# Splitting attention weights in place, three mean passes in the head, and ScalarE as a second reader of the mask words

## The chip, the cores and the metric

The kernel runs on 1 core of one Trainium2 chip. The metric is the device time of one execution in microseconds; the times are given as the median of several executions, and one more execution was taken with the hardware profiler. TensorE is called PE, VectorE DVE, ScalarE ACT, GpSimd POOL and SyncE SP, as in the profile.

## The reference

Two graph attention layers over N = 4096 nodes with F = 64 features and one dense 4096 x 4096 integer adjacency matrix, nearly empty (the diagonal and about one entry in a thousand):

```python
def layer(h, a, slope):                   # layer 2 first does h = h @ W
    e = (h @ a[:64])[:, None] + (h @ a[64:])[None, :]
    e = leaky_relu(e, slope)              # 0.01 in layer 1, 0.2 in layer 2
    p = softmax(where(adj > 0, e, -9e15), axis=1)
    return p @ h                          # layer 2 adds elu() on this
x = layernorm(x + layer1(x)); out = layernorm(x + layer2(x))
```

## The kernel before

The exponential of a leaky sum is a product of a factor of the row and a factor of the column, one pair of factors for positive sums and one for negative ones. So each layer is a product of a 0/1 matrix (mask and sign) with weighted feature rows, done once for each sign and combined per row. The matrix is made from signs: ACT writes sign(s_i + d_j) as one byte, DVE masks it with an AND (`negative`, L831) and an XOR (`positive`, L842).

**Tiling.** A supertile `q` is 512 rows (4 tiles `t` of 128), and there are `NQ` = 8 of them in each layer. A step `k` (8 in each supertile) takes 4 chunks `b` of 128 columns. In a step, ACT makes four rows of signs (`compare`, L670), DVE does `negative` and `positive`, and PE does 32 matmuls (`products`, L1223): 4 tiles by 4 chunks by 2 signs, each with a 128x128 fp8 stationary block and a moving block of 195 bf16 columns. PE accumulates a whole supertile in four PSUM banks `acc`.

Layers and supertiles are counted from 1 in the text and steps, groups and tiles from 0; the code counts all from 0, so its `weigh(1, 0)` is group 0 of layer 2.

**Words.** In layer 1 the adjacency has to be turned first. POOL issues its loads (L490) into `enc`, PE turns one step's four blocks into the PSUM tile `tb` (`turn_masks`, L1147), two steps ahead and in the middle of `products`, and DVE copies them to `mask_t` (`extract`, L757), one step ahead. Layer 2 finds all words in `mask_t`. `look` (L742) checks the words for values that are not 0 or 1.

**Weights.** Chunk values `val` (64 features and a one) are multiplied by the column's two factors to 520 f32 products for each group of four chunks, by POOL (`multiply`, L328), for group 7 of layer 2 by DVE. Each product is kept as three bf16 parts. The f32 word's upper half is the first part; DVE subtracts it (`weigh`, L814), the rest's upper half is the second part, and DVE subtracts that and writes the third part (L820). ACT copies the first two (`keep_parts`, L626, one copy of 1040 bf16; POOL's L554 for the last group). All three land side by side in `wmov`, in the order sign, part, column; this is what the matmuls read. The products lie in scratch (`split` and borrowed places) that two groups share in turn, so `multiply` waits for DVE and ACT two groups back. Group g of layer 2 may be written to `wmov` only when the last supertile of layer 1 has done step g (`mm_done`). Two groups are made earlier, staged in the unused end of `mask_t` and moved by two DMAs of SP (`move_weights`, L456); `extract` in the last supertile waits for these before it writes over the end.

**Queues.** Every engine runs a list written out by hand. In supertile 1 of layer 1, DVE's step k is: `negative(k)`, `positive(k)`, `extract(k+1)`, the two halves of `weigh(k+1)`, then small work: `sum_s` at k = 1, `set_scur` at k = 2, `clip_s` at k = 4. POOL's `multiply(g)` there waits for `positive(g-2)`, counted by `poss`. PE's mean of x (`mean_pass`, L1262) is one matmul of 512 f32 columns in the middle of steps 1, 2, 4 and 5 each; DVE reduces the result (`take_mean`, L908) in step 0 of supertile 2. A supertile's sums are read from PSUM by DVE (`sum_parts`, L857) in step 0 of the next one; the epilogue after them is POOL's, and DVE's at the change of layers. `positive(k)` waits until step k-2 is done on PE (two buffers), `compare(k)` for k-4 (four buffers).

Of the kernel before, what the change touches and what calls it, by code (L numbers as in the profile page):

```python
# [5 lines left out]
P = 128  # L6
N = 4096
F = 64
NQ = 8
TI = 4  # L10
KB = 8
NB = 4
ROWS = TI * P
KP = 2
# [3 lines left out]
FD = F + 1  # L18
# [13 lines left out]
STAGED = 2  # L32
# [3 lines left out]
WEIGH = 2  # L36
XP = 4
MEAN_STEPS = (1, 2, 4, 5)
# [14 lines left out]
def fast_attention(nc, x, adj, a0, w1, a1, x1_dram, out, flag, stored):  # L53
# [7 lines left out]
    with ExitStack() as ctx:  # L61
# [12 lines left out]
        enc = sb("enc", [P, NU, TI, UW], F32)  # L74
# [3 lines left out]
        wmov = sb("wmov", [P, KB * NB, 2 * WC], BF16)  # L78
        vsum = sb("vsum", [P, 2, F], F32)
        val = sb("val", [P, KB * NB, FD], F32)  # L80
        split = sb("split", [P, NB, 2, 2, FD], F32)
# [5 lines left out]
        ones = sb("ones", [P, 1], F32)  # L87
        share = sb("share", [P, 1], F32)
# [12 lines left out]
        strange = sb("strange", [P, 1], F32)  # L101
# [9 lines left out]
        def spare(q, half):  # L111
# [8 lines left out]
        s_prod, d_prod, x_chunks = spare(NQ - 1, 1), spare(NQ - 2, 0), spare(NQ - 2, 1)  # L120
# [28 lines left out]
        moved = [sem(f"moved{i}") for i in range(STAGED)]  # L149
        looked = sem("looked")  # L150
        turned = sem("turned")
        masked = sem("masked")
        rows_turned = sem("rows_turned")
# [14 lines left out]
        w_prod = [sem(f"w_prod{i}") for i in range(2)]  # L168
        w_vec = sem("w_vec")
        w_act = sem("w_act")  # L170
        w_pool = sem("w_pool")
# [35 lines left out]
        lots = NB * 2 * 2 * FD  # L207
        other_split = [flat[:, 0:lots].rearrange("p (b s r c) -> p b s r c", b=NB, s=2, r=2) for flat in (
            mask_t[:, NQ - 3].rearrange("p k t i -> p (k t i)").bitcast(F32),
            enc[:, 1:3].rearrange("p u t j -> p (u t j)"))]  # L210

        last_words = mask_t[:, NQ - 1].rearrange("p k t i -> p (k t i)").bitcast(F32)
        staged_split = last_words[:, 0:lots].rearrange("p (b s r c) -> p b s r c", b=NB, s=2, r=2)
        staged_words = last_words.bitcast(BF16)
        first_staged = 2 * KB * TI * P - STAGED * NB * 2 * WC

        def staged(g):

            c0 = first_staged + g * NB * 2 * WC
            return staged_words[:, c0:c0 + NB * 2 * WC]  # L220

        def steps_of(g):

            c0 = first_staged + g * NB * 2 * WC
            return range(c0 // (2 * TI * P), (c0 + NB * 2 * WC - 1) // (2 * TI * P) + 1)

        def is_staged(layer, g):
            return layer == 1 and g < STAGED

        def parts_of(layer, g):  # L230

            if g % 2 == 0:
                return split[:, :, :, :, :]
            return staged_split if is_staged(layer, g) else other_split[layer]

        def weights_of(layer, g):

            if is_staged(layer, g):
                return staged(g).rearrange("p (b c) -> p b c", b=NB)
            return wmov[:, NB * g:NB * g + NB]  # L240

        def top_of(layer, g):

            return parts_of(layer, g).rearrange("p b s r c -> p (b s r c)").bitcast(BF16)\
                .rearrange("p (b s r c h) -> p b s r c h", b=NB, s=2, r=2, h=2)[:, :, :, :, :, 1]

        lone_mean = enc[:, 0, 0, :].rearrange("p (t d) -> p t d", d=F)
        enc8 = enc[:, :, :, :].bitcast(FP8)
# [61 lines left out]

        def multiply(eng, ops, layer, g):

            n = NQ * layer + g
            cs = slice(NB * g, NB * g + NB)
            if layer == 1:

                eng.wait_ge(grp_set, 3 * (g + 1))
                eng.wait_ge(b_set, 4 if g < EARLY else 2 * (g - EARLY) + 6)
                if g % 2 and not is_staged(1, g):
                    eng.wait_ge(turned, KB * (NQ - 1) + 6)  # L320
            elif g:

                eng.wait_ge(poss, max(g - 1, 1))

            if n > 1:
# [1339 lines left out]
```

## Time and profile before

| | |
|---|---|
| median of 3 executions | 437.58 us (437.0 to 438.23) |
| the profiled execution's own time | 437.87 us |
| its span from first to last instruction | 436.0 us |
| busy in the span: PE / DVE / ACT / POOL | 406.4 / 380.3 / 382.9 / 252.2 us |
| granted TensorE clock, mean | 0.992 |

The span is the part that the profile shows; 1.87 us of the execution lie around it. A busy share alone does not say what bounds a stage, because the stages differ: the head and the change of layers have work that the steady supertiles don't have.

### The profile page before, as it was taken

To read this page: it belongs to the slowest core of one execution; us is meant where nothing else is said; L and a number is where in the kernel's file an instruction comes from. 1 tells how busy PE (TensorE), PEld (TensorE's weight loads), DVE (VectorE), ACT (ScalarE), POOL (GpSimd) and SP (SyncE) were. 2 spreads that over 40 slices of the span, in tenths; PEclk is the share of its full clock that TensorE was granted. 3 is DMA by queue.
4 is the path that set the end of the run, shared out by engine and by line. 5 is a ranking of instruction groups with operands and counts; after the bars stand their busy time and mean duration, and the time that the engine had idled before them with its cause. 6 is when DMAs were issued, how large, how long until landed. Compare 5 with 4: busy or idle time off the path is not lost.

```text
span 436.0 us, 11844 instructions
## 1 busy us (share of the span) xinstructions
PE 406.4 (93%) x4484; PEld 397.8 (91%) x4484; DVE 380.3 (87%) x683; ACT 382.9 (88%) x590; POOL 252.2 (58%) x292
## 2 busy tenths in 40 slices
PE   1599999999999999999999999999999999999980
PEld 1388999999999999999998998999999999999980
DVE  4799998899898989999889997689999999999963
ACT  3899986979979799779998989999999999999930
POOL 5533353753738547296493135568696969695931
PEclk9999999999999999999999999999999999999996
DMA  5999989799897998988610000000000000000000
GB/s 118 99 107 108 90 75 98 68 101 80 78 102 66 95 85 73 90 73 88 83 52 1 2 26 2 2 26 2 27 2 26 0 24 1 24 2 26 2 26 17
DMA packets 22766, 22.48 MB, mean 52 GB/s; under 512 B 1344, under 2 KB 22464, under 8 KB 22720
## 3 DMA queue, kind: packets, MB, share of 16 engines
q0 software_dynamic: 17424, 16.78, 44.4%
q1 hardware_dynamic: 4208, 4.05, 2.9%
q10 hardware_dynamic: 1088, 1.05, 0.7%
q8 instruction: 28, 0.46, 0.4%
q14 instruction: 18, 0.15, 0.1%
HBM read 69.30 MB, written 2.10 MB: 164 GB/s over the span
## 4 chain that ended last, share of the span: by engine, by line
PE 75%; DVE 15%; issue 6%; POOL 1%; DMA 1%; ACT 0%; DVEq 0%; POOLq 0%
PE acc L1223 67%; PE tb L1147 5%; DVE neg L831 3%; DVE pos L842 3%; DVE mask_t L757 2%; PE srcb L1157 1%; DMA mask_t<-in_x 1%; DVE split L814 1%; DVE mask_t L814 1%; PE pg L1191 1%; DVE scr L857 1%; DVE wmov L820 1%; DVE mask_t L913 1%; DVE dcol L921 1%; DVE enc L814 1%
## 5 line engine op out<-in xcount | busy, mean ns | idle before, releaser
L670 ACT ACTIVATE neg<-srcb,dcol 128x512 int8<-128x512 f32 x512 | 358.2, 973 | 4.4 <-PE acc L1223 4.0
L1223 PE MATMUL acc<-wmov,pos 128*128 128x195 bf16 x2016 | 357.1, 248 | 3.6 <-DVE pos L842 2.6
L1223 PE MATMUL acc<-wmov,neg 128*128 128x195 bf16 x2016 | 357.3, 249 | 0.0
L1223 PEld LDWEIGHTS acc<-wmov,pos 128*128 128x128 fp8e4 x2016 | 198.5, 98 | 7.6 <-DVE pos L842 5.6
L1223 PEld LDWEIGHTS acc<-wmov,neg 128*128 128x128 fp8e4 x2016 | 197.5, 98 | 2.3 <-issue 1.3
L842 DVE TENSOR_TENSOR pos<-neg,mask_t 128x1024 uint16<-128x1024 uint16 x128 | 104.8, 819 | 15.3 <-DVE neg L831 1.6
L831 DVE TENSOR_TENSOR neg<-neg,mask_t 128x1024 uint16<-128x1024 uint16 x128 | 102.9, 804 | 10.8 <-ACT neg L670 8.0
L490 POOL DMA_DIRECT2D enc<-in_adj x31 | 24.7, 798 | 63.5 <-DVE scr L857 31.1
L757 DVE TENSOR_SCALAR mask_t<-tb 128x512 uint32<-128x512 uint32 (+1 forms) x64 | 43.9, 686 | 6.7 <-PE tb L1147 6.0
L1147 PE MATMUL tb<-ident,enc 128*128 128x128 f32 x256 | 39.5, 278 | 2.7 <-DMA enc<-in_adj 2.7
L742 DVE SCALAR_TENSOR_TENSOR odd<-mask_t,odd 128x1024 uint32<-128x1024 uint32 x32 | 38.8, 1213 | 0.0
L857 DVE TENSOR_REDUCE scr<-acc 128x130 f32<-128x390 f32 x60 | 31.7, 557 | 1.4 <-PE acc L1223 0.2
L1147 PEld LDWEIGHTS tb<-ident,enc 128*128 128x128 f32 x256 | 29.1, 143 | 3.5 <-DMA enc<-in_adj 3.3
L345 POOL TENSOR_TENSOR scr<-scr,acol 128x260 f32<-128x260 f32 x14 | 13.0, 926 | 30.0 <-issue 23.3
L404 POOL TENSOR_SCALAR small<-mv 128x4 f32<-128x4 f32 x14 | 9.1, 652 | 19.2 <-DVE mv L875 19.0
L407 POOL TENSOR_TENSOR small<-small 128x4 f32<-128x4 f32 x14 | 19.3, 1382 | 1.2
L328 POOL TENSOR_TENSOR split<-val,bcol 128x520 f32<-128x520 f32 x8 | 9.0, 1125 | 14.5 <-DVE scr L392 12.3
L347 POOL TENSOR_TENSOR scr<-scr,acol 128x260 f32<-128x260 f32 x14 | 14.9, 1065 | 0.0
L366 POOL TENSOR_TENSOR scr<-scr 128x256 f32<-128x256 f32 x14 | 13.5, 963 | 1.1
L421 POOL TENSOR_TENSOR xout<-scr,small 128x256 f32<-128x256 f32 x14 | 13.1, 937 | 1.1
L350 POOL TENSOR_TENSOR scr<-scr 128x260 f32<-128x260 f32 x14 | 13.0, 930 | 1.1
L635 ACT COPY xt<-pg 128x256 f32<-128x256 f32 x8 | 3.4, 421 | 11.0 <-PE pg L1183 11.0
(139 smaller groups left out, 301.7 us busy)
## 6 DMA issues: line engine op xcount, KB each, us to landing
enc<-in_adj POOLq DMA_DIRECT2D x31, 512.0 KB, 8.2
mask_t<-in_x ACTq DMA_DIRECT2D x4, 256.0 KB, 5.7
x_rows<-xout SPq DMA_DIRECT2D x8, 128.0 KB, 3.1
resid<-x_rows SPq DMA_DIRECT2D x8, 128.0 KB, 2.1
out<-xout SPq DMA_DIRECT2D x8, 128.0 KB, 1.7
wmov<-mask_t SPq DMA_DIRECT2D x2, 390.0 KB, 3.4
enc<-in_adj POOLq DMA_DIRECT2D x2, 256.0 KB, 8.3
resid<-in_a SPq DMA_DIRECT2D x1, 64.0 KB, 4.6
```

The lines of the kernel that those rows point to most:

```text
L347: ops.tensor_tensor(tmp, part[:, :, 1, :], wide(acol[:, layer, 1, q, :], FD), ALU.mult)\
L366: ops.tensor_tensor(numf, numf, tmpf, ALU.add).then_inc(done, 1)
L407: ops.tensor_tensor(rstd, var, mhalf, ALU.pow).then_inc(done, 1)
L490: nc.gpsimd.dma_start(enc8[:, u, :, :], adj_v[q, u]).then_inc(adj_landed[u], 16)
L670: ins = nc.scalar.activation(neg[:, k % SR, :, b], srcb[:, q % 2, :], ACT.Sign, bias=dcol[:, layer, c:c + 1])
L742: nc.vector.scalar_tensor_tensor(odd[:, :], mask_pairs[:, n, :], NOT_BINARY, odd[:, :], ALU.bitwise_and, ALU.bitwise_or).then_inc(looked, 1)
L757: nc.vector.tensor_scalar(mask_t[:, q, k, :, :], tb[:, :, :].bitcast(U32), WORD, None, ALU.bitwise_and).then_inc(masked, 1)
L831: nc.vector.tensor_tensor(neg16[:, k % SR, :], neg16[:, k % SR, :], bits, ALU.bitwise_and)\
L842: nc.vector.tensor_tensor(pos16[:, k % MR, :], neg16[:, k % SR, :], bits, ALU.bitwise_xor)\
L857: nc.vector.tensor_reduce(part[:, t, :, :], acc[t][:, 0:2 * WC].rearrange("p (s r c) -> p s c r", s=2, r=SPLIT), AX.X, ALU.add).then_inc(a ...
L1147: ins = nc.tensor.transpose(tb[:, t, :], enc[:, k // KP, t, k % KP * P:(k % KP + 1) * P], ident[:, :])
L1223: ins = nc.tensor.matmul(acc[t][:, side * WC:(side + 1) * WC], m[:, t * P:(t + 1) * P, b], wmov[:, c, side * WC:(side + 1) * WC], start=fi ...
```

## The change

- **In place.** The products of a group get an eight-byte slot each: the f32 product and, beside it, the f32 rest. The slot's four bf16 halves are then: waste, first part, third part, second part. `weigh` writes the third part into the lower half of the rest, and the matmuls read halves 1 to 3 of each slot in place: a moving operand of 65 runs of three bf16 with a step of eight bytes, instead of 195 side by side. In PSUM the order becomes sign, column, part, still without gaps, and `sum_parts` reads three neighbours. `wmov`, `split`, `keep_parts` (ACT, 15 copies), POOL's copy and the two DMAs of SP are gone, and the waits with them. Each group has a home of its own: `wts`, `apart_wts`, the end of `mask_t`, or a slot of `enc_lots` (`wait_for_home` says when a home is free). `weigh(1, 0)` moves from step 4 to step 5 of supertile 7, `weigh(1, 1)` from step 6 of supertile 7 to step 2 of supertile 8, and POOL's `multiply(1, 1)` from step 5 to step 7 of supertile 7.
- **Mean.** The four passes go to bank 1 of `srcb`: one at PE's very start, one before `turn_stat`, one between the first two `turn_masks`, and one in step 1. `take_mean` goes to step 2 of supertile 1; `spread_rows` of supertile 2 waits for it.
- **Words by ACT.** In supertile 1 the words of steps 3, 5 and 7 are copied by ACT right after the signs of the same step, as 1024 uint16 each (before, all were DVE's). Those who wait for words there count two semaphores.

```diff
-                        else:
-                            keep_parts(0, k - 1)
+                        if k in BY_ACT:
+                            extract(k)
...
+            def extract(k):
+
+                act.wait_ge(turned, k + 1)
+                nc.scalar.copy(mask_t[:, 0, k, :, :].rearrange("p t i -> p (t i)").bitcast(U16),
+                               tb[:, :, :].rearrange("p t i -> p (t i)").bitcast(U16)).then_inc(masked_act, 1)
...
-                dve.wait_ge(w_prod[g % 2], n // 2 + 1)
-                nc.vector.tensor_tensor(rest, both[:, :, :, 0, :], top[:, :, :, 0, :], ALU.subtract)\
-                    .then_inc(w_vec, 1)
-                if layer == 1 and not is_staged(1, g):
-
-                    dve.wait_ge(mm_done, KB * (NQ - 1) + g + 1)
+                both, halves = parts_of(layer, g), halves_of(layer, g)
+                product, rest = both[:, :, :, :, 0], both[:, :, :, :, 1]
+
+                dve.wait_ge(w_prod, n + 1)
+                nc.vector.tensor_tensor(rest, product, halves[:, :, :, :, 1], ALU.subtract).then_inc(w_vec, 1)
+
                 dve.wait_ge(w_vec, WEIGH * n + 1)
-                nc.vector.tensor_tensor(w[:, :, :, 2, :], rest, top[:, :, :, 1, :], ALU.subtract)\
+                nc.vector.tensor_tensor(halves[:, :, :, :, 2], rest, halves[:, :, :, :, 3], ALU.subtract)\
...
-                acc[t][:, side * WC:(side + 1) * WC], m[:, t * P:(t + 1) * P, b],
-                                wmov[:, c, side * WC:(side + 1) * WC], start=first, stop=last, skip_group_check=True)
+                acc[t][:, side * WC:(side + 1) * WC].rearrange("p (c r) -> p c r", r=SPLIT),
+                            m[:, t * P:(t + 1) * P, b],
+                                moving(layer, k, b, side), start=first, stop=last, skip_group_check=True)
...
+            def halves_of(layer, g):
+
+                return home(layer, g).bitcast(BF16).rearrange("p (b s c h) -> p b s c h", b=NB, s=2, h=4)
+
+            def moving(layer, g, b, side):
+
+                return halves_of(layer, g)[:, b, side, :, 1:4]
...
+            def mean_pass(h):
+
+                pe.wait_ge(x_landed[h], 16)
+                ins = nc.tensor.matmul(srcb[:, 1, :], share[:, :].broadcast_to([P, P]),
+                                       x_chunks[:, h * piece:(h + 1) * piece], start=h == 0, stop=h == XP - 1)
```

## Rows read from the trace of the kernel before

**Rows 1.** The page's costliest groups: busy, mean ns, idle before and its releaser.

```profile
L1223 PE MATMUL acc<-wmov,pos 128*128 128x195 bf16 x2016 | 357.1, 248 | 3.6 <-DVE pos L842 2.6
L857 DVE TENSOR_REDUCE scr<-acc 128x130 f32<-128x390 f32 x60 | 31.7, 557 | 1.4 <-PE acc L1223 0.2
```

**Rows 2.** Busy time of the engines by stretch (length, then PE, PEld, DVE, ACT, POOL).

```profile
24.00:54.00 30.00, 29.87 (x305) 27.28 (x302) 28.81 (x46) 28.84 (x42) 10.33 (x12) 1.00 1.08 101
224.00:263.00 39.00, 36.44 (x401) 34.62 (x399) 35.96 (x69) 36.36 (x62) 13.07 (x15) 1.00 0.04 12
266.00:415.00 149.00, 148.96 (x1716) 148.55 (x1715) 134.59 (x223) 148.29 (x222) 112.13 (x115) 1.00 0.04 12
```

**Rows 3.** The chain that ended last: start, us, what.

```profile
56.48 1.05 DVE pos L842
...
274.62 22.14 PE acc L1223 x256
```

**Rows 4.** Timeline of DVE, supertile 1 and the start of supertile 2.

```profile
27.28 0.69 DVE L842 TENSOR_TENSOR pos<-neg,mask_t 128x1024 uint16<-128x1024 uint16 x1
27.89 0.68 DVE L757 TENSOR_SCALAR mask_t<-tb 128x512 uint32<-128x512 uint32 x1
28.49 1.20 DVE L814 TENSOR_TENSOR mask_t<-mask_t 128x520 f32<-128x520 f32 x1
29.72 0.70 DVE L820 TENSOR_TENSOR wmov<-mask_t 128x520 bf16<-128x520 f32 x1
...
51.69 0.68 DVE L908 TENSOR_REDUCE meanv<-pg 128x64 f32<-128x512 f32 x1
...
55.29 1.09 DVE L831 TENSOR_TENSOR neg<-neg,mask_t 128x1024 uint16<-128x1024 uint16 x1
56.48 1.03 DVE L842 TENSOR_TENSOR pos<-neg,mask_t 128x1024 uint16<-128x1024 uint16 x1
```

**Rows 5.** Timeline of POOL in the same stretch.

```profile
28.07 1.06 POOL L328 TENSOR_TENSOR split<-val,bcol 128x520 f32<-128x520 f32 x1 [0.79 <-DVE pos L842]
...
55.22 0.61 POOL L363 TENSOR_TENSOR scr<-small,meanv 128x256 f32<-128x256 f32 x1
55.91 1.06 POOL L366 TENSOR_TENSOR scr<-scr 128x256 f32<-128x256 f32 x1
```

**Rows 6.** Timeline of PE in the head.

```profile
12.57 0.37 PE L1163 MATMUL pg<-ident,stat 128*1 128x128 f32 x1 [1.61 <-DVE stat L765]
...
22.16 0.80 PE L1147 MATMUL tb<-ident,enc 128*128 128x128 f32 x4 [0.53 <-DMA enc<-in_adj]
...
26.01 1.02 PE L1262 MATMUL pg<-mask_t,share 128*128 128x512 f32 x2
26.87 0.25 PE L1223 MATMUL acc<-wmov,pos 128*128 128x195 bf16 x1
...
54.12 0.26 PE L1223 MATMUL acc<-wmov,pos 128*128 128x195 bf16 x1 [0.25 <-DVE pos L842]
```

**Rows 7.** Timeline of ACT in the head.

```profile
33.63 1.07 ACT L626 COPY wmov<-split 128x1040 bf16<-128x1040 bf16 x1
```

**Rows 8.** Timeline of DVE at the change of layers.

```profile
220.53 0.69 DVE L757 TENSOR_SCALAR mask_t<-tb 128x512 uint32<-128x512 uint32 x1 [0.53 <-PE tb L1147]
224.16 0.69 DVE L757 TENSOR_SCALAR mask_t<-tb 128x512 uint32<-128x512 uint32 x1 [0.38 <-PE tb L1147]
233.26 1.23 DVE L814 TENSOR_TENSOR split<-split 128x520 f32<-128x520 f32 x1
259.10 1.57 DVE L820 TENSOR_TENSOR wmov<-enc 128x520 bf16<-128x520 f32 x1
```

**Rows 9.** Timeline of POOL and PE at the change of layers.

```profile
232.87 1.07 POOL L328 TENSOR_TENSOR enc<-val,bcol 128x520 f32<-128x520 f32 x1 [2.88 <-ACT wmov L626]
259.06 1.06 POOL L554 COPY wmov<-enc 128x1040 bf16<-128x1040 bf16 x1 [7.22 <-DVE enc L814]
262.41 0.26 PE L1223 MATMUL acc<-wmov,pos 128*128 128x195 bf16 x1 [0.54 <-DVE pos L842]
```

More of the change, by code:

```diff
@@ L86, in fast_attention @@
         ident = sb("ident", [P, P], F32)
-        ones = sb("ones", [P, 1], F32)
-        share = sb("share", [P, 1], F32)
+        single = sb("single", [P, 3], F32)
+        ones, share, strange = (single[:, i:i + 1] for i in range(3))
         att1 = sb("att1", [F, 2], F32)
@@ L167, in fast_attention @@
         a_set = sem("a_set")
-        w_prod = [sem(f"w_prod{i}") for i in range(2)]
+        w_prod = sem("w_prod")
         w_vec = sem("w_vec")
-        w_act = sem("w_act")
-        w_pool = sem("w_pool")
         limits = sem("limits")
@@ L236, in weights_of @@
[L236 to L248, printed above, removed]
+        first_tail = KB * TI * P - TAIL * LOT
@@ new lines, in home, with wait_for_home @@
+        def home(layer, g):
+            if layer == 0 and g < TAIL:
+                flat = last_words[:, first_tail + g * LOT:first_tail + (g + 1) * LOT]
+            elif layer == 0:
+                flat = wts[:, g - TAIL]
+            else:
+                flat = {0: apart_wts[:, :], 1: enc_lots[:, 0], 2: enc_lots[:, 1], 3: wts[:, 0], 4: wts[:, 1],
+                        5: wts[:, 2], 6: enc_lots[:, 2], 7: enc_lots[:, 3]}[g]
+            return flat
+        def wait_for_home(eng, g):
+            if g in (1, 2, 6, 7):
+                lot = {1: 0, 2: 1, 6: 2, 7: 3}[g]
+                eng.wait_ge(turned, KB * (NQ - 1) + KP * (lot + 1))
+            elif g:
+                eng.wait_ge(mm_done, KB * (NQ - 1) + g)
@@ L309, in before, with wait_for_words @@
             return layer, q - 1, NQ * layer + q - 1
+        def wait_for_words(eng, n):
+            if isinstance(n, int) and n <= KB:
+                by_act = sum(k < n for k in BY_ACT)
+                eng.wait_ge(masked, n - by_act)
+                if by_act:
+                    eng.wait_ge(masked_act, by_act)
+            else:
+                eng.wait_ge(masked, n - len(BY_ACT))
         def multiply(eng, ops, layer, g):
-            n = NQ * layer + g
             cs = slice(NB * g, NB * g + NB)
@@ L906, in take_mean @@
                 dve.wait_ge(mean_ps, layer + 1)
-                shares = pg[:, :] if layer == 0 else pg[:, 0:2 * F]
+                shares = srcb[:, 1, :] if layer == 0 else pg[:, 0:2 * F]
                 nc.vector.tensor_reduce(meanv[:, :], shares.rearrange("p (c f) -> p f c", f=F), AX.X, ALU.add)\
@@ L997, in body @@
                         sum_parts(*done, range(0, TI // 2))
-                    if ahead(layer, q, k, 1):
+                    if ahead(layer, q, k, 1) and not (layer == 0 and is_first(q) and k + 1 in BY_ACT):
                         extract(*ahead(layer, q, k, 1))
@@ L1025, in body @@
                             sum_s(1, 2, 2)
+                        if k == 2:
+                            take_mean(0)
                         if k == 4:
@@ L1200, in products @@
                 apart(pe, q)
[L1201 to L1204 removed]
+                if is_first(q):
                     pe.wait_ge(w_vec, WEIGH * (NQ * layer + k + 1))
[L1207 to L1210 removed]
                 for t in range(TI):
```

149 lines of the change are left out of this document (43 added, 106 removed).

## The prediction, on record before the changed kernel was run

> **What bounds the kernel now.** I read the page's groups first. A matmul of `products` has a mean of 248 ns [rows 1], but matmuls overlap, so their pace is read elsewhere: in the chain 256 of them take 22.14 us [rows 3], which is 86.5 ns each. There are 2 x 8 x 8 x 32 = 4096 of them, 354 us of a span of 436. Busy time by stretch says where PE is not the bound [rows 2]: from 266 to 415 us it idles 0.04 us in 149, but from 224 to 263, the change of layers, 2.56 us in 39. The steady supertiles give nothing unless the matmul itself gets faster or slower.
>
> The head is less plain. From 24 to 54 us PE is busy for 29.87 of 30 us [rows 2], yet the chain runs on DVE up to a `positive` that ends at 57.53 [rows 3] and only then turns to PE. Both hold: PE has four mean passes there, and DVE ends each `positive` only shortly before PE is free. At 54.12 PE is the one that waits, 0.25 us for DVE [rows 6]. So the head has two bounds almost level, and taking work off one gains only what the other allows.
>
> DVE's own step in the head is lengthened by POOL. After `positive(2)` (end 27.97) come `extract` (0.60 from start to start), then L814, which starts at 28.49 and takes 1.20 us, then L820, 0.70 [rows 4]. POOL's `multiply` runs from 28.07 to 29.13 [rows 5]. L814 ends at 29.69, 0.56 after POOL: it was held until POOL was done. Two instructions later in the head show the turn-taking. `negative` at 55.29 ends at 56.38, 0.55 after L363's end; L366, wanted from 55.83, ends 0.59 after `negative`; `positive`, wanted from 56.48, ends 0.54 after L366 [rows 4, 5]. DVE with two inputs in SBUF and POOL alternate, each holding the other off for a whole instruction, even where DVE's next instruction follows within 0.1 us. `extract` reads PSUM and isn't held (0.68 us under a running POOL).
>
> **The change, part by part.** The sum is made against the profiled execution, 437.87 us; the median of the three is 0.29 lower.
>
> *The moving operand.* No row shows one with gaps. From below the cost is nothing; a gain is excluded, since the columns stay 195. From above: the operand now crosses 65 x 8 = 520 bytes instead of 390, so if bytes crossed set the pace, 86.5 becomes 115.3 ns and 4096 matmuls cost 118 us more. The nearest row is TensorE's other read: the stationary block takes one byte of every four, so it crosses 512 bytes in each 86.5 ns, and it keeps up (its column PEld has as many instructions as PE, [rows 2]). I take nothing. The Trainium skill (SBUF — State Buffer, section Door 1: The DMA port swizzle) says that SBUF is read in lines of 16 bytes and that two or more reads in a line keep full rate, so that bf16 may step up to 8 elements for free; here a line gives six of its eight halves. By that rule the term is 0 as well, where the bound by bytes says 118 us; no run here shows it yet.
>
> *DVE's operands* get steps of eight bytes. Nothing in the rows has that form either. L814 now runs 520 elements in about 0.61 us, one element a cycle, and already reads every other half; I take no change. The bound from above is doubling: 0.6 us for each of two halves of 16 groups, of which the groups on the path (8 in the head, 5 at the change) would cost 15 us. `sum_parts` reads neighbours instead of a step of 65; its 557 ns for 390 elements [rows 1] is again about one a cycle, so 0.
>
> *ACT.* Each copy that leaves is 1.07 us [rows 7], 15 in all with eight in the head. What comes is three copies of 1024 elements from PSUM, about 1.1 us each by the same row. ACT gets 8 x 1.07 - 3 x 1.1 = 5.3 us lighter in the head, and none of that is on the path: `negative` isn't waiting for signs there. `extract(3)` on ACT must wait for PE's turn in the middle of step 1 (26.2), ends near 27.3, and its words are wanted by `negative(3)` at 30.4. What is queued behind it on ACT is `compare(4)`, done by 30.2 and wanted at 34.3. Covered; were ACT late, each copy would cost its 1.1.
>
> *DVE in the head.* Three extracts leave: 3 x 0.60 = 1.80 at steps 2, 4 and 6. But at steps 2 and 4 `multiply(4)` and `multiply(6)` are released by the `positive` just before, and the extract was the cover for 0.6 us of it. Without it: L814 from 27.99 to 28.60, POOL's turn to 29.6, L820 to 30.2, where today it ends at 30.34. That is 0.1 instead of 0.6, twice. At step 6 no multiply is left, and the full 0.6 comes. Sum 0.8. Against it: `negative` of steps 3 to 7 waits for a third semaphore. A gap between DVE instructions grows from about 0.02 to 0.08 with a second wait (28.49 + 1.20 to 29.72, against `negative` to `positive`, 56.38 to 56.48, [rows 4]), so 5 x 0.05 = 0.25. `take_mean` costs 0.60 at step 2 and gives back 0.60 in supertile 2 (51.69, [rows 4]), both on DVE's chain. DVE's net at 57.5: 0.8 - 0.25 = 0.55 earlier.
>
> *PE in the head.* A pass is 0.86 us (26.01 to 26.87, [rows 6]). Three leave the stretch: 2.58. The one before `turn_stat` lies in the 1.61 us that PE idled before 12.57 [rows 6]. Even at twice its later length, 1.7 us, it would end 0.1 after that idle; PE's small matmuls there may also run faster for the work before them and give 0.1 back; I take 0. The pass between the first turns is hidden: what is late there is the adjacency's DMA, for which PE waits again at 22.16 [rows 6]. With 2.58 less, PE stands free at each `positive` from step 2 on, and DVE alone decides: head 0.55 to 0.65 faster. I take **0.6**.
>
> *The change of layers.* `weigh(1, 1)` moves into supertile 8 at step 2: 0.62 + 0.62 = 1.24, and 0.4 for one POOL turn (its epilogue runs there). DVE idles 0.53 at 220.53 and 0.38 at 224.16 for PE's turns [rows 8], and without two ACT copies in supertile 7 it starts the supertile some 0.25 earlier. So 1.64 - 1.16 = 0.48 late. `multiply(1, 5)` no longer waits 2.88 us for ACT's copy [rows 9]; it comes right behind `multiply(1, 4)` and holds L820 of group 3 for about 0.87, where today it holds L814 of group 4 for 0.54 (1.23 at 233.26, [rows 8]): 0.33 late. Four L820 lose a second wait, 4 x 0.06 = 0.24 early. At the end POOL's copy goes: it held L820 of group 7 for 0.87 (1.57 at 259.10, [rows 8, 9]), and PE idled 0.54 before 262.41 [rows 9]. The two adds behind it (0.6 each) move up to 256.8 and can hold L328, at most 0.5. So 0.54 back. Sum 0.48 + 0.33 - 0.24 - 0.54 = +0.13, against a bound of -2.56 if all of PE's idling went. SP's two DMAs and the waits for them go too: they landed long before `extract` asked. The new waits of `extract` in supertile 8 (its steps 0 and 1 done) are met by two steps.
>
> Sum: 437.87 - 0.6 + 0.1 = 437.4 for a profiled execution, **437.1** as a median.
>
> **The rivals.** *DVE keeps its turn.* If L820, 0.02 us behind L814, goes ahead of the waiting POOL, steps 2 and 4 save 1.1 each. With step 6 that is 2.8, less 0.6 until the mean is given back; then PE's own work bounds the head, and its 2.58 is the most it can give. About 2.2: 437.87 - 2.2 + 0.1 - 0.29 = 435.5. For it: the gap is smaller than the 0.1 of the pair above. Against it: POOL took its turn in those rows every time. Chance 0.24.
>
> *DVE has no slack in supertile 8.* The 1.16 us of absorption don't come, because POOL's epilogue is late by as much as it is held, and DVE waits for it instead. Then 1.64 + 0.33 - 0.24 - 0.54 = +1.2 there, less 0.6: 438.2. It ends above before as soon as more than 0.6 arrives at PE. For it: PE idles 2.56 us in 224 to 263 because DVE is the chain there. Chance 0.17.
>
> *The gaps in the moving operand cost.* Each ns is 4.1 us; half a ns outweighs all else. The bound is 437.6 + 118 = 555. Chance 0.06.
>
> *Nothing comes.* The head gives nothing because the early waits (mean before `spread_rows`, the words' two counts) take it back: 437.6. Chance 0.08.
>
> **How the numbers follow.** My forecast has 0.45. What a measurement here can tell from no change is 0.3%, 1.3 us. Faster by more: the first rival and a little of the forecast's lower end, 0.28. Slower by more: the operand's 0.06 and the upper half of the second rival, 0.15. Within: 0.57. The range runs from 435.0 (first rival, with a few tenths of the idle at the change) to 438.8 (second rival with a POOL turn more); only the operand's case and the far ends lie outside, under 2 in 10. The forecast's own range is 436.4 to 437.8.
>
> **What would show it.** Matmuls of `products` 86.5 ns apart in the steady supertiles (not so: the third rival). At steps 2 and 4 of supertile 1, L820 about 1.65 us long behind a short L814 (0.7 would be the first rival). One mean pass of 0.86 us in step 1 and none later; PE idling a few tenths before several steps of supertile 1. The first full PE stretch of layer 1 starting at about 57.0 instead of 57.5. In supertile 8, DVE's idling of 0.53 and 0.38 gone, PE's idling at about 229 and 236 grown by tenths, and no idling before step 7 of supertile 9. Wrong would be above all: a turn order between DVE and POOL unlike that of [rows 4, 5], or slower two-input instructions through the eight-byte steps.

## The result and the profile after

The changed kernel takes 535.29 us (median of 4 executions, 534.82 to 536.22), the one before 437.29 beside it: a ratio of 1.223 [1.220, 1.226], slower by 98 us. I had forecast 437.1. The case that came is the third rival, the gaps in the moving operand, which had 0.06. The profiled execution took 536.22 us with a span of 534.2.

The page's busy row and its groups, in the form of [rows 1]:

```profile
PE 511.7 (96%) x4484; PEld 444.1 (83%) x4484; DVE 384.3 (72%) x680; ACT 381.9 (71%) x578; POOL 243.8 (46%) x291
L1179 PE MATMUL acc<-wts,pos 128*128 128x195 bf16 x1152 | 261.7, 272 | 0.7 <-DVE pos L803 0.6
...
L803 DVE TENSOR_TENSOR pos<-neg,mask_t 128x1024 uint16<-128x1024 uint16 x128 | 98.3, 768 | 70.4 <-PE acc L1179 62.4
...
L818 DVE TENSOR_REDUCE scr<-acc 128x130 f32<-128x390 f32 x60 | 33.6, 564 | 14.3 <-PE acc L1179 14.0
```

`products` (now L1179) goes from a mean of 248 to 272 ns. DVE and ACT are as busy as before in us and less in share: `positive` idles 70.4 us, 62.4 of it for PE. `sum_parts` (L818), which now reads neighbours, has 564 ns against 557.

Windows of the kernel after: the head, steady supertiles of layer 1, and steady supertiles of layer 2 (columns as in [rows 2]).

```profile
24.00:54.00 30.00, 29.48 (x253) 24.60 (x251) 28.78 (x39) 21.79 (x32) 8.53 (x8) 0.99 1.00 92
58.00:224.00 166.00, 166.00 (x1491) 147.66 (x1489) 120.01 (x211) 117.35 (x183) 72.89 (x93) 1.00 0.75 68
275.00:330.00 55.00, 54.53 (x487) 47.40 (x486) 43.98 (x84) 42.31 (x73) 16.64 (x20) 1.00 0.02 6
```

PE is never idle in 166 us, at a granted clock of 1.00, its higher level of 2.4 GHz. So neither a wait nor the clock has slowed it there: the matmuls themselves take longer. In the head the clock did fall once, after PE had idled 1.89 us before its first product at 19.65:

```profile
21.00:24.00 3.00, 3.00 (x19) 2.41 (x17) 2.96 (x3) 2.27 (x4) 1.58 (x2) 0.50 1.11 105
```

0.50 is the lower level of 1.2 GHz, and matmuls are 165 ns apart in it. PE waited for DVE again later, at 38.96 and 47.62, so what the lower clock cost was made up by then. The chain says how much longer a matmul takes.

Chain of the kernel after, against [rows 3]:

```profile
46.87 0.70 DVE pos L803
...
47.62 1.96 PE acc L1179 x16
...
270.54 0.69 DVE mask_t L722
...
288.10 0.57 DVE scr L818
...
388.23 28.63 PE acc L1179 x256
```

256 matmuls take 28.63 us, 111.8 ns each, where before they took 22.14, or 86.5. The difference is 25.35 ns. For all 4096 it is 103.8 us; 98 arrived. PE becomes the chain at 47.6 instead of 57.5, and it keeps it up to 270.5; at the change of layers DVE has most of it until 288.7.

Where the 98 arose is read from the starts of `spread_rows` in step 3 of each supertile, one mark in each (PE timeline of both kernels; supertile 16 has none):

| stretch | before, us | after, us | difference |
|---|---|---|---|
| start to the mark of supertile 2 | 60.79 | 67.71 | 6.9 |
| six periods of layer 1, mark to mark | 26.74 to 27.26 | 33.24 to 33.77 | 39.1 in all |
| change of layers, two periods | 52.31 | 61.82 | 9.5 |
| five periods of layer 2 | 22.58 to 22.78 | 29.07 | 32.2 in all |
| last mark to the end | 48.9 | 59.4 | 10.5 |

A steady supertile takes 6.5 us more, and 256 x 25.35 ns is 6.49: nothing but the matmul's pace has changed there. The head's stretch holds some 368 matmuls, 9.3 us by count, and the change of layers 512, 13.0 us. They grow by less, 6.9 and 9.5, because PE was not the bound in all of them before.

DVE and POOL in the head, timelines of the kernel after, against [rows 4, 5]:

```profile
25.60 1.19 DVE L778 TENSOR_TENSOR wts<-wts 128x520 f32<-128x520 f32 x1
26.82 1.33 DVE L781 TENSOR_TENSOR wts<-wts 128x520 bf16<-128x520 f32 x1
...
29.17 0.69 DVE L803 TENSOR_TENSOR pos<-neg,mask_t 128x1024 uint16<-128x1024 uint16 x1
29.78 0.70 DVE L778 TENSOR_TENSOR wts<-wts 128x520 f32<-128x520 f32 x1
30.51 2.08 DVE L781 TENSOR_TENSOR wts<-wts 128x520 bf16<-128x520 f32 x1
32.39 0.66 DVE L869 TENSOR_REDUCE meanv<-srcb 128x64 f32<-128x512 f32 x1
```

```profile
25.16 1.07 POOL L326 TENSOR_TENSOR wts<-val,bcol 128x520 f32<-128x520 f32 x1 [2.56 <-DVE pos L803]
...
29.95 1.45 POOL L326 TENSOR_TENSOR wts<-val,bcol 128x520 f32<-128x520 f32 x1 [1.30 <-DVE pos L803]
```

Read POOL's row at 29.95 first. It ends at 31.40, and L781, though only 0.03 us behind L778, ends at 32.59: POOL had its turn between the two halves, as forecast. But L781 needs 1.2 us after POOL's end, where before a half needed 0.56 [rows 4, 5]. At 26.82 no product of POOL lies beside it, and it still takes 1.33 against 0.70. The next instruction starts before a row's end, so the start-to-start times are shorter: 1.13 against 0.62. So a second cost came that I had put at nothing.

PE and ACT in the head, against [rows 6, 7]:

```profile
12.81 0.42 PE L1128 MATMUL pg<-ident,stat 128*1 128x128 f32 x1
...
15.02 1.92 PE L1215 MATMUL srcb<-mask_t,single 128*128 128x512 f32 x2
```

```profile
27.58 1.01 ACT L623 COPY mask_t<-tb 128x1024 uint16<-128x1024 uint16 x1 [4.31 <-PE tb L1110]
```

The pass put before `turn_stat` makes that 0.24 us late (12.81 for 12.57, I had bounded it at 0.1). Such an early pass takes PE 1.7 to 1.9 us from its start to the next instruction's, against 0.86 later. ACT's copy of the words takes 1.01, against my 1.1.

### The profile page after: what moved, and what is told of

Same layout as the page of the kernel before. It is cut to its first block, busy times and chain, and to the rows that moved or that the text cites. A ratio compares the mean times of both kernels' runs of the same rounds, so it can differ in the third digit from the quotient of the medians.

```text
span 534.2 us, 11824 instructions
## 1 busy us (share of the span) xinstructions
PE 511.7 (96%) x4484; PEld 444.1 (83%) x4484; DVE 384.3 (72%) x680; ACT 381.9 (71%) x578; POOL 243.8 (46%) x291
## 4 chain that ended last, share of the span: by engine, by line
PE 84%; DVE 7%; issue 5%; POOL 1%; DMA 1%; ACT 1%; ACTq 0%; POOLq 0%; DVEq 0%
PE acc L1179 77%; PE tb L1110 4%; DVE pos L803 2%; DVE neg L792 1%; DVE wts L778 1%; PE srcb L1122 1%; DMA mask_t<-in_x 1%; DVE mask_t L722 1%; PE pg L1154 1%; POOL mask_t L326 0%; PE srcb L1215 0%; DVE wts L781 0%; PE pg L1146 0%; DVE mask_t L778 0%; ACT L577 0%
## 5 line engine op out<-in xcount | busy, mean ns | idle before, releaser
L1179 PE MATMUL acc<-wts,pos 128*128 128x195 bf16 x1152 | 261.7, 272 | 0.7 <-DVE pos L803 0.6
L1179 PE MATMUL acc<-wts,neg 128*128 128x195 bf16 x1152 | 261.8, 275 | 0.0
L803 DVE TENSOR_TENSOR pos<-neg,mask_t 128x1024 uint16<-128x1024 uint16 x128 | 98.3, 768 | 70.4 <-PE acc L1179 62.4
L1179 PEld LDWEIGHTS acc<-wts,pos 128*128 128x128 fp8e4 x1152 | 113.0, 98 | 16.5 <-DVE pos L803 2.0
L1179 PEld LDWEIGHTS acc<-wts,neg 128*128 128x128 fp8e4 x1152 | 111.4, 97 | 17.8
L1179 PE MATMUL acc<-enc_lots,neg 128*128 128x195 bf16 x480 | 108.1, 275 | 0.0
L1179 PE MATMUL acc<-enc_lots,pos 128*128 128x195 bf16 x480 | 108.1, 272 | 0.0
L1179 PE MATMUL acc<-mask_t,pos 128*128 128x195 bf16 x256 | 59.4, 275 | 1.9 <-DVE pos L803 1.9
L1179 PE MATMUL acc<-mask_t,neg 128*128 128x195 bf16 x256 | 59.4, 277 | 0.0
L1179 PEld LDWEIGHTS acc<-enc_lots,neg 128*128 128x128 fp8e4 x480 | 46.4, 97 | 7.5
L1179 PEld LDWEIGHTS acc<-enc_lots,pos 128*128 128x128 fp8e4 x480 | 47.0, 98 | 6.4
L818 DVE TENSOR_REDUCE scr<-acc 128x130 f32<-128x390 f32 x60 | 33.6, 564 | 14.3 <-PE acc L1179 14.0
L1179 PEld LDWEIGHTS acc<-mask_t,pos 128*128 128x128 fp8e4 x256 | 25.4, 99 | 6.2 <-DVE pos L803 2.6
```

The lines of the kernel that those rows point to most:

```text
L803: nc.vector.tensor_tensor(pos16[:, k % MR, :], neg16[:, k % SR, :], bits, ALU.bitwise_xor)\
L818: nc.vector.tensor_reduce(part[:, t, :, :], acc[t][:, 0:2 * WC].rearrange("p (s c r) -> p s c r", s=2, r=SPLIT), AX.X, ALU.add).then_inc(a ...
L1179: ins = nc.tensor.matmul(acc[t][:, side * WC:(side + 1) * WC].rearrange("p (c r) -> p c r", r=SPLIT), m[:, t * P:(t + 1) * P, b], moving(l ...
```

## The experiments

My theory after the result had two parts: the gaps in the moving operand cost 25 ns a matmul, and the eight-byte step costs `weigh` some 0.6 us a group (by its rows). The rival for the first was that the place of the weights (`wts`, `enc_lots`) or the order in PSUM does it, not the gaps.

**e1_dense: the changed kernel, but the matmuls read 195 halves side by side.**

```diff
-                return halves_of(layer, g)[:, b, side, :, 1:4]
+                return fixed[:, side * WC:(side + 1) * WC].rearrange("p (c r) -> p c r", r=SPLIT)
```

> The changed kernel, with one thing different in the timed path: every matmul of products reads its 195 bf16 columns side by side from one pair of dense blocks (words of the mask, so the sums are meaningless; the parts are still all made and waited for), and the flag for the general path is held at 0. If the gaps in the moving operand are what costs, the pace goes from 111.8 ns back to 86.5 ns and the whole to about 437 to 439 us (the changed kernel's 535.3 less 4096 x 25.3 ns = 103.6 would be 431.7, but PE's idling at the head and the change of layers, absorbed now, comes back; my sum without the operand's term was 437.1). If instead the new homes of the weights, the order in PSUM or anything else of the change slows the matmuls, the pace stays near 111.8 ns and the time near 535 us.

440.70 us, ratio to before 1.0065 [1.0044, 1.0086]. Its PE timeline in layer 2, every eighth row:

```profile
337.04 0.25 PE L1180 MATMUL acc<-mask_t,neg 128*128 128x195 bf16 x1
...
337.72 0.25 PE L1180 MATMUL acc<-mask_t,neg 128*128 128x195 bf16 x1
```

Eight matmuls in 0.68 us are 85.0 ns each. The form of the read alone is worth 94.6 us; the places of the weights, PSUM's order and all else stayed. By count it would be 4096 x 26.8 ns, 109.8 us; the rest is lost where PE isn't the bound in e1: in the head, at the change of layers, and by some tenths in each supertile of layer 2 (22.62 us, with 21.76 of matmuls). In layer 2 e1's chain is mostly ACT's `compare` (L649), so there the faster read can't show in full. What remains, 2.9 us above before, I put down to `weigh` (e7 tests it): the same 2.08 us as after,

```profile
30.33 2.08 DVE L782 TENSOR_TENSOR wts<-wts 128x520 bf16<-128x520 f32 x1
```

**e2_forms: eight forms of the moving operand, one for each step, and eight forms of what `weigh`'s second half writes, one for each group of layer 1.**

```diff
+FORMS = ((0, 3, 3, 65), (1, 3, 3, 65), (1, 3, 4, 65), (0, 3, 4, 65), (1, 3, 8, 65), (2, 2, 4, 98), (1, 2, 4, 98),
+         (1, 1, 2, 195))
...
-            return halves_of(layer, g)[:, b, side, :, 1:4]
+            start, run, step, runs = FORMS[g]
+            if run == step:
+                return fixed[:, start:start + run * runs].rearrange("p (c r) -> p c r", r=run)
+            return fixed[:, 0:step * runs].rearrange("p (c h) -> p c h", h=step)[:, :, start:start + run]
```

> The changed kernel as a probe: in each step k the matmuls read the moving operand in another form, from a block of finite words, so the sums are meaningless. k0: 195 side by side. k1: the same from an odd half. k2: the change's form, runs of 3 at half 1, step 8 bytes. k3: runs of 3 at half 0. k4: as k2, step 16 bytes. k5: 98 runs of 2 at half 2 (one word of 4 bytes), step 8 bytes. k6: 98 runs of 2 at half 1 (astride two words). k7: single halves, step 4 bytes. Theory of words (one aligned word of four bytes in each 0.83 ns, two bf16 if both are wanted): k0 and k1 86.5 ns, k2 to k4 111.8, k5 86.5, k6 and k7 about 166. Theory of bytes crossed: k2, k3 111.8, k4 about 220, k5 to k7 166. Theory of runs (two neighbours of a run in a cycle, wherever they start): as words, but k6 86.5. VectorE's second half of weigh in layer 1 also differs by group: 0 and 7 as in the change (1.23 us net of POOL's turns), 1 writes f32 in place, 2 bf16 side by side, 3 bf16 with a step of 4 bytes, 4 bf16 with a step of 8 bytes in another place, 5 the same in upper halves, 6 in place but subtracting a half of another word. If bf16 writes with gaps cost, 3 to 6 are slow, 1 and 2 take 0.62; if writing into the slot that is read costs, 1 is slow, 2 to 5 fast; if reading rest and its own half at once costs, only 6 is fast.

One execution, 475.3 us. PE timeline in step 7 (195 single halves, every other one) and in step 2 (the change's form), eight matmuls apart:

```profile
359.75 0.25 PE L1194 MATMUL acc<-mask_t,pos 128*128 128x195 bf16 x1
...
360.45 0.25 PE L1194 MATMUL acc<-mask_t,pos 128*128 128x195 bf16 x1
...
366.90 0.28 PE L1194 MATMUL acc<-mask_t,pos 128*128 128x195 bf16 x1
...
367.79 0.28 PE L1194 MATMUL acc<-mask_t,pos 128*128 128x195 bf16 x1
```

0.70 us for eight against 0.89; over whole steps 86.7 ns against 110.8. Step 7 crosses 780 bytes and touches 195 words, yet runs at 86.7 ns; the change's form crosses 520 bytes. That ends the theories by bytes crossed and by words touched, and the one by runs as I had stated it, since none gave step 7 full pace. All paces are in the table below.

What `weigh`'s second half writes shows on DVE: bf16 side by side (group 2), bf16 with a step of four bytes (group 3), bf16 with a step of eight in another tile (group 4):

```profile
25.69 0.70 DVE L796 TENSOR_TENSOR apart_wts<-wts 128x520 bf16<-128x520 f32 x1
...
28.89 1.52 DVE L796 TENSOR_TENSOR apart_wts<-wts 128x520 bf16<-128x520 f32 x1
...
34.19 1.33 DVE L796 TENSOR_TENSOR apart_wts<-wts 128x520 bf16<-128x520 f32 x1
```

and on POOL beside group 3:

```profile
28.34 1.45 POOL L332 TENSOR_TENSOR wts<-val,bcol 128x520 f32<-128x520 f32 x1 [1.25 <-DVE pos L818]
```

POOL ends at 29.79 and DVE's row at 30.41, 0.62 later, where a dense half ended 0.56 and the change's 1.19 after POOL: a step of four bytes costs almost nothing. Group 4 takes 1.33, with no POOL beside it. The first half of `weigh` writes f32 with the same eight-byte step in 0.70, and group 1, whose second half writes f32 in place, has 1.65 for the change's 2.32 (both held by POOL), so writing into the slot that is read is not the cause. Group 6, which subtracts a half of another word, still takes 1.34, so reading the rest and its own half at once is not either. It is the bf16 write with a step of eight bytes that is slow, wherever it lands (groups 0 and 4 to 7; the upper halves too).

**e3_mean and e4_words: before, with only the mean's passes moved; before, with only the words by ACT.** Their edits are those parts of the diff, on the kernel before:

```diff
-                shares = pg[:, :] if layer == 0 else pg[:, 0:2 * F]
+                shares = srcb[:, 1, :] if layer == 0 else pg[:, 0:2 * F]
...
+            mean_pass(0)
...
+                        if layer == 0 and is_first(q) and k == 1:
+                            mean_pass(3)
```

```diff
+BY_ACT = (3, 5, 7)
...
+                        if k in BY_ACT:
+                            extract(k)
...
-                    if ahead(layer, q, k, 1):
+                    if ahead(layer, q, k, 1) and not (layer == 0 and is_first(q) and k + 1 in BY_ACT):
```

> The kernel before with the mean's part of the change alone: four passes at PE's start, before turn_stat, between the first turns and in step 1, in bank 1 of srcb; take_mean in step 2 of supertile 1. By my sum PE loses three passes (2.58 us) from the stretch where it is never idle, but DVE bounds the head and take_mean only moves: 0 to 0.3 us faster, 437.0 to 437.3. The rival that PE is the bound there says up to 2.5 us faster, 434.8. The rival that the early passes delay turn_stat or the first turns says 0.2 to 0.6 us slower.

> The kernel before with ScalarE taking the words of steps 3, 5 and 7 in supertile 1, and nothing else; keep_parts stays. By my sum DVE gains 0.1 + 0.1 + 0.6 less 0.25 for extra waits = 0.55 us, and PE with its mean passes still in place allows about 0.2 of it: 437.1. The rival says ScalarE, which still has the copies of keep_parts in the head (3.85 us a step for a step of 3.75 to 4.2), becomes the bound with 1.0 us more in three steps: 1 to 2 us slower, 438.3 to 439.3.

437.18 us, ratio 0.9985 [0.9970, 1.0001], and 437.42, ratio 0.9997 [0.9982, 1.0012]. Neither can be told from no change. With the mean moved, PE's busy time in the head falls from the 29.87 of [rows 2], and DVE's does not:

```profile
24.00:54.00 30.00, 28.23 (x302) 26.46 (x300) 28.81 (x45) 28.27 (x41) 9.84 (x11) 1.00 1.07 100
```

PE's busy time falls by 1.64 us, and the head ends no earlier. Chain of e3's head:

```profile
43.85 0.70 DVE pos L841
44.59 1.56 PE acc L1222 x16
```

DVE has the chain up to step 6, and comes there 0.8 us later than before (43.85 for 43.06): `take_mean`, 0.68 us, now lies in it, and step 1 starts a quarter of a us later, behind the early passes. From 44.6 on PE has it without a pause. So each bound has a part of the head. In e4 ACT already shares the chain (`compare`, `keep_parts` and the words' copy, from 42.0 to 47.8): its rival's mechanism came, its 1 to 2 us did not.

**e5_turned: the same slots and the same halves, read part by part: three runs of 65 with a step of eight bytes inside.**

```diff
-            return halves_of(layer, g)[:, b, side, :, 1:4]
+            return halves_of(layer, g)[:, b, side, :, 1:4].rearrange("p c r -> p r c")
```

> The changed kernel with one thing different: a matmul reads the same three halves of the same 8-byte slots in the order part, column (3 runs of 65 with a step of 8 bytes) instead of column, part (65 runs of 3); PSUM is in the order sign, part, column again, as before the change. The same 520 bytes are crossed. The rule that the forms probe suggests, two columns in a cycle of 0.83 ns as long as both are in the innermost run, gives 3 x 33 = 99 cycles instead of 65 x 2 = 130 (dense: 98): 86 to 87.5 ns a matmul, and 441 to 444 us. If instead the gaps or the eight-byte step are the price, the pace stays at 111.8 ns or more and the time at 535 us or above.

802.27 us, ratio 1.833 [1.828, 1.839]. The chain:

```profile
622.39 45.53 PE acc L1179 x256
```

177.8 ns each. I had expected a cure and got the worst form of all. What it pointed to is a second limit: the order in which the same bytes are read decides how often a part of the memory is visited, and here each piece of 16 bytes is entered three times, once for each part.

**e6_planes: the parts of a group in planes of 65, four bytes from column to column, three runs of 65.**

```diff
-            return halves_of(layer, g)[:, b, side, :, 1:4]
+            h = halves_of(layer, g)[:, b, side, 1:2]
+            return bass.AP(h.tensor, h.offset, [h.ap[0], [FD, SPLIT], [2, FD]])
...
-                nc.vector.tensor_tensor(halves[:, :, :, :, 2], rest, halves[:, :, :, :, 3], ALU.subtract)\
+                nc.vector.tensor_tensor(third, rest, second, ALU.subtract)\
```

> The whole change, with the parts kept in planes: 65 products and 65 rests of a chunk and sign one after the other, the third part written into free lower halves so that the three parts start 65 halves apart; a matmul reads 3 runs of 65 with a step of 4 bytes, and all of DVE's operands have steps of 4 bytes. Against the turned kernel this takes away DVE's slow write (1.23 us instead of 0.62, in 16 groups, some 13 of them on DVE's chain in the head and at the change of layers). If both prices are gone, my sum for the rest of the change comes due: 437.1, within 436.4 and 438.5. If a cycle more per matmul (99 against 98) costs 0.83 ns, 3.4 us come on top: 440.5. If a write with a step of 4 bytes is slow here too, 441 to 444.

459.94 us, ratio 1.051 [1.048, 1.054]. It is in place too, and 75 us faster than the change. Its chain and its `weigh`, whose third part now has a step of four bytes:

```profile
359.30 23.84 PE acc L1183 x256
```

```profile
25.23 0.77 DVE L785 TENSOR_TENSOR wts<-wts 128x520 bf16<-128x520 f32 x1
```

93.1 ns, and 0.77 where the change has 1.33. The write is cured and the read only in part; by the paces, 27 us of the read's cost are left, of which 22.5 arrived. None of the three cases that I expected has this.

**e7_dense_planes: e6's writes with e1's dense read**, so without the cost of the change's read and almost without that of its write.

> As the first dense probe (the matmuls read mask words side by side, sums meaningless, flag held at 0), but with the planes for what DVE and POOL write. The difference to that probe (440.7) is the price of DVE's slow write alone: by 0.61 us in each group on DVE's chain, up to 8 in the head and 3 to 5 at the change of layers, 3 to 6 us less, of which PE's own work in the head lets through about half: 437 to 438.5. If the write isn't what made that probe 2.9 us slower than before, it stays at 440.7.

434.63 us, ratio 0.9925 [0.9900, 0.9951]. Against e1 it is 6.1 us less, all of it in the head (mark of supertile 2 at 59.38 for 63.37) and at the change of layers (53.72 for 56.55): the price of the slow write where DVE is the chain (6.8 by these marks of the two profiled executions, of which 0.6 are lost again after the last mark). DVE and POOL at step 2 of supertile 1:

```profile
27.69 0.69 DVE L782 TENSOR_TENSOR wts<-wts 128x520 f32<-128x520 f32 x1
28.42 1.52 DVE L785 TENSOR_TENSOR wts<-wts 128x520 bf16<-128x520 f32 x1
```

```profile
27.86 1.45 POOL L327 TENSOR_TENSOR wts<-val,bcol 128x520 f32<-128x520 f32 x1 [1.27 <-DVE pos L807]
```

L782 starts 0.8 us earlier than its counterpart L814 in [rows 4], runs 0.69, then POOL's turn holds L785. I forecast 27.99 to 28.60, POOL to 29.6 and the second half to 30.2; the rows say 27.69 to 28.38, 29.31 and 29.94. The rival in which DVE keeps its turn did not come.

The ratio flatters: this read runs at 85.0 ns, not at 86.5. Six periods of layer 1 are 0.37 us shorter each for that, 2.2 us, and the head by up to 0.5. Without these two the kernel would stand near 437.3. If the pace also shortened the change of layers (512 matmuls, 0.8 us) and the stretch behind the last mark (0.5), it would stand near 438.6; both are estimates from the marks, and before beside it stands at 437.44. Layer 2's supertiles are no shorter than before, because ACT bounds them:

```profile
275.00:330.00 55.00, 54.16 (x631) 53.45 (x630) 48.29 (x84) 55.00 (x84) 39.38 (x40) 1.00 0.04 11
```

ACT is busy for all of the 55 us, as it is in the kernel before. No in-place form tried reaches this pace; the kernel is a probe, since its matmuls don't read the weights.

**e8_mean_words: before, with e3's and e4's edits together.**

> The kernel before with two of the three parts of the change: the mean's passes in the head and ScalarE's three copies of words, and not the weights in place. Alone they gave 0.15% (-0.3 to +0.01) and 0.03% (-0.18 to +0.12). If each frees what bounds the other (PE's passes, DVE's extracts), together they give more than the sum: 436.2 to 436.8 (my 0.55 to 0.65 for the head, and more if DVE keeps its turn). If ScalarE, still with keep_parts, is the bound: no better than the mean alone, 437.0.

437.35 us, ratio 0.9994 [0.9977, 1.0010]. Chain of its head:

```profile
35.10 1.00 ACT mask_t L662
36.10 2.80 ACT neg L687 x4
38.91 0.90 ACT wmov L637
...
44.60 2.77 ACT neg L687 x4
47.37 0.92 ACT wmov L637
...
48.42 1.54 PE acc L1242 x16
```

While `keep_parts` exists, three copies of words more make ACT the third bound of the head. The in-place part is what would have made room for the other two: in e7, without `keep_parts`, ACT is busy for 25.69 us from 24 to 54, in e8 for 29.46.

**e9_forms2: eight more forms of the moving operand**, to try two limits drawn from the paces so far. First, two columns are read in 0.83 ns only if both are in the same innermost run, so a run of three takes two such steps; 3.3 ns come on top. Second, each line of 16 bytes that is entered costs 1.8 ns. The slower of the two sets the pace.

```diff
+FORMS = ((0, 65, 65, 3, 1), (1, 5, 6, 39, 1), (0, 65, 66, 3, 1), (1, 3, 16, 63, 1), (2, 2, 8, 98, 1), (0, 195, 1, 1, 3),
+         (1, 65, 65, 3, 2), (1, 65, 136, 3, 2))
```

> A second probe of the moving operand's form, by step as before (sums meaningless, flag held at 0). Two limits are to be tried, drawn from the forms, turned and planes runs: A, two columns in a cycle of 0.83 ns, only out of the same innermost run, plus 3.3 ns a matmul; B, 1.8 ns for each 16 bytes that are entered. The slower one sets the pace. k0: 195 side by side, starts 390 bytes apart as in wmov: A 85.0. k1: 39 runs of 5, step 12 bytes: A 117 cycles, 100.8; B 53. k2: 3 dense runs of 65, step 132 bytes: A 85.8. k3: 63 runs of 3, step 32 bytes: A 126 cycles, 108; B 63 x 1.8 = 113; a limit by bytes crossed (9 a ns) would give 224. k4: 98 runs of 2, step 16 bytes: B 176, A 85. k5: 195 single halves, step 6 bytes: B 73 x 1.8 = 131. k6: 3 runs of 65 single halves with a step of 4 bytes, starts 130 bytes apart (as planes): B 51 x 1.8 = 92, measured 93. k7: the same, starts 272 bytes apart: 92.

One execution, 525.44 us. Steps 3, 4 and 5 on PE, eight matmuls apart:

```profile
353.48 0.28 PE L1186 MATMUL acc<-mask_t,neg 128*128 128x189 bf16 x1
...
354.39 0.27 PE L1186 MATMUL acc<-mask_t,neg 128*128 128x189 bf16 x1
...
385.33 0.36 PE L1186 MATMUL acc<-mask_t,pos 128*128 128x196 bf16 x1
...
386.74 0.36 PE L1186 MATMUL acc<-mask_t,pos 128*128 128x196 bf16 x1
...
390.32 0.29 PE L1186 MATMUL acc<-mask_t,pos 128*128 128x195 bf16 x1
...
391.36 0.29 PE L1186 MATMUL acc<-mask_t,pos 128*128 128x195 bf16 x1
```

All forms of e2 and e9, with the changed kernel, e5 and e6; the two limits are worked out as above:

| moving operand | run limit, ns | lines | line limit, ns | measured, ns |
|---|---|---|---|---|
| side by side, 1 run of 195 | 85.0 | 25 | 45 | 84.2 to 86.5 |
| 3 runs of 65 side by side, starts 132 bytes apart | 85.8 | 27 | 49 | 85.0 |
| singles, step 4 bytes (1 run of 195) | 85.0 | 49 | 88 | 86.7 |
| singles, step 6 bytes (1 run of 195) | 85.0 | 73 | 131 | 129 to 130 |
| 98 runs of 2, step 8 | 85.0 | 49 | 88 | 86.7 |
| 98 runs of 2, step 16 | 85.0 | 98 | 176 | 175 to 176 |
| 39 runs of 5, step 12 | 100.8 | 30 | 54 | 100.8 |
| 65 runs of 3, step 8 (the change) | 111.6 | 33 | 59 | 110.8 to 111.8 |
| 65 runs of 3, step 16 | 111.6 | 65 | 117 | 115.6 |
| 63 runs of 3, step 32 | 108.3 | 63 | 113 | 113.3 |
| 3 runs of 65, step 4 inside (e6) | 85.8 | 51 | 92 | 93.1 |
| the same, starts 272 bytes apart | 85.8 | 51 | 92 | 90.0 |
| 3 runs of 65, step 8 inside (e5) | 85.8 | 99 | 178 | 177.8 |

The sizes are a fit. 0.83 ns for two columns comes from the differences: 19 steps more than dense cost 15.8 ns (runs of 5), 32 more cost 26.8 (the change). 1.8 ns a line is 175.6 over 98 lines. That the unit is 16 bytes is shown by two rows: 98 runs of 2 with a step of 8 and of 16 bytes would enter 98 pieces of 8 bytes alike but take 86.7 and 176 ns, and with pieces of 32 bytes the step of 16 would have 49 entries and that of 32 would have 63, but they take 176 and 113 ns. All eight forms of e9 were expected in numbers before they ran, and every one came within 2 ns. Within that the fit is not exact: the three side-by-side runs of 65 should have cost 0.8 ns more than one run and cost nothing more, forms with 49 lines are 1.5 ns faster than their limit, and where the rows start moves the pace by 1 to 3 ns (84.2 to 86.5, 90.0 and 93.1).

**e10_mean_word7: before, with the mean moved and only step 7's words by ACT** (`BY_ACT = (7,)`), to see whether one copy still fits.

> The kernel before with the mean's passes in the head and only one of ScalarE's three copies of words, that of step 7, for which DVE has no turn of POOL to wait for. With all three copies the chain of the head ran on ScalarE (keep_parts still there); with none it ran on PE from step 6 on. So DVE's 0.6 us at step 6 should give nothing (PE is the bound from there) and ScalarE should stay off the chain: as the mean alone, 437.2, within 0.3. The rival says that ScalarE is the bound again with one copy of 1.0 us: 437.5 or more; or that DVE still counts: 436.6.

437.23 us, ratio 0.9984 [0.9969, 0.9999]: the interval just leaves out no change, and allows 0.3% at most. The time is the one I expected, and the path is not: from 34.4 to 48.0 the chain of its head is again ACT's (`compare`, `keep_parts`), where I had expected ACT to stay off it. No version that computes the reference beats the kernel before by more than 0.3%.

## Why the prediction was wrong

**The moving operand: the step that failed.** I took its term as nothing; it measured 25.35 ns a matmul, 103.8 us by count, of which 94.6 show between the changed kernel and e1. The argument rested on the nearest row, the stationary block, which crosses 512 bytes in 86.5 ns with one byte of four. That row is of another read. The stationary block steps evenly, one element at a time. The moving operand has an inner run of three, and by the forms it is the odd run that costs: pairs don't reach across runs (98 runs of 2 take 86.7 ns, 65 runs of 3 take 111.8). An even step of four bytes costs next to nothing here as well (86.7 ns). So the row was right and did not bear on the form in question.

The bound from above, 115.3 ns by bytes crossed, came near 111.8 by luck: e2's step 7 crosses more bytes at full pace. Both ends were known, half a ns outweighed all else in the sum, and I gave the upper one 0.06.

The Trainium skill (SBUF — State Buffer, section Door 1: The DMA port swizzle) allows bf16 a step of up to 8 elements. The runs contradict it for this read: a step of 3 elements costs 45 ns a matmul (130 against 85), the step of 4 in e5's three runs costs 93, and the change's own form, free by that rule, costs 25.35. What they do bear out is the line of 16 bytes as the unit, at 1.8 ns for each one entered.

**DVE's operands: the second step that failed.** I took no change, from a row that *reads* every other half. The cost is in the write: from start to start 0.62 becomes 1.13 for bf16 with a step of eight bytes, in each of 16 groups (0.66 with a step of four, in e6 and e7). I had a doubling as the bound, for both halves; one half nearly has it. Between e1 and e7 it is worth 6.1 us, and 13 groups at 1.13 - 0.66 are 6.1 too; my bound of 15 counted both halves. What it costs in the changed kernel no run takes apart; PE is busy there for 29.48 of the 30 us from 24 to 54, so little of it can show in the head.

**DVE in the head.** POOL's turn between the halves came at steps 2 and 4, at step 2 with times within 0.3 us of the forecast (e7). ACT's copies are covered only because `keep_parts` is gone; e8 shows that otherwise they are not.

**PE in the head.** Three passes leave and nothing comes by itself, as the two level bounds said: e3 has its mark of supertile 2 at 60.76 against 60.79. But I had DVE alone decide from step 2 on, and in e3 PE has the chain from 44.6 on, in step 6. The pass before `turn_stat` cost 0.24, not 0.

**Head and change of layers together.** With both failed terms out (e7), the head is 1.4 us shorter, about 0.9 without the probe's faster pace, where I said 0.6. The change of layers is 1.4 longer, up to 2.2 at the pace of before, where I said 0.13 (and the four terms that I added there, 0.48 + 0.33 - 0.24 - 0.54, make 0.03). My slack did not hold there: in e7 PE idles for DVE in supertile 8,

```profile
227.17 0.26 PE L1183 MATMUL acc<-mask_t,pos 128*128 128x195 bf16 x1 [1.18 <-DVE pos L807]
```

with DVE held by POOL's products, three of them back to back where the kernel before has two (at 226.99 and 228.47):

```profile
225.05 4.47 POOL L327 TENSOR_TENSOR wts<-val,bcol 128x520 f32<-128x520 f32 x3
```

PE also idles 0.79 us before 219.50, behind the moved `weigh(1, 1)`. That is the second rival's mechanism, DVE without slack in supertile 8, larger than I priced it (its case had +1.2). Which of the moved steps brings POOL's products together was not tried apart. The rest of my sum, 437.1, thus has two sizes wrong in opposite directions. By e7 it is between 437.3 and 438.6, and where it comes near my number, that is luck.

What stays open: why a bf16 write with an eight-byte step nearly halves DVE's rate; why the read of `wmov` runs at 86.5 ns and dense reads at other starts at 85.0 (the same starts as `wmov`'s gave 86.1 in e9, so the starts are part of it); and how much of e7's correction for that is exact.

## What to carry to other kernels

Before packing operands so that one engine saves a copy, count what the most frequent reader pays: here 4096 matmuls read what 15 copies had laid out, and 1 ns of pace was worth 4.1 us. Write the moving operand's access as runs and lines: here a short odd inner run lost half a pair each time, and every 16-byte line entered had a price, so the same bytes in another order took 1.6 times as long (177.8 ns for 111.8). And ask what bounds each stage once the bound engine gets faster: a matmul 1.5 ns faster gave nothing in layer 2, where ACT was level with PE. When no row shows the form of an access and its upper bound is larger than everything else in the sum, the width of the range and the chance must follow that bound, not the likeness of a neighbouring row.

## What the runs showed of the hardware that was not expected

- TensorE's moving read of bf16 has two limits, for this shape: some 0.83 ns for two columns of one innermost run, and 1.8 ns for each 16-byte line entered (a fit, within 2 ns of all forms tried). Runs of 3, of 5 and of 2 columns gave 111, 101 and 87 ns; 49, 73 and 98 lines gave 87, 130 and 176.
- VectorE's subtraction with 520 bf16 written takes from start to start 0.62 us side by side, 0.66 with a step of four bytes and 1.13 with a step of eight (rows of 0.70, 0.77 and 1.33); f32 with a step of eight has rows of 0.69 to 0.70, as the dense write has.
- VectorE reading two inputs from SBUF lets a waiting POOL instruction in, even when its own next instruction is 0.03 us behind: in the kernel after at 30.5, in e7 at 28.4.
